# Last layer of a graph network: rows fetched by TensorE from two float32r terms, and for one block of edges in twelve

## What is computed

```python
def _L1_gnn_ref(nodes, edge_index, edge_features, mw1, mb1, uw1, ub1, uw2, ub2):
    ...
    src, dst = (edge_index[0], edge_index[1])
    msg_in = jnp.concatenate([nodes[src], edge_features], axis=1)
    messages = jax.nn.silu(msg_in @ mw1 + mb1)
    aggregated = jax.ops.segment_sum(messages, dst, num_segments=nodes.shape[0])
    upd_in = jnp.concatenate([nodes, aggregated], axis=1)
    updated = jax.nn.silu(upd_in @ uw1 + ub1) @ uw2 + ub2
    return nodes + updated
```

## Time and profile before

| what | us |
| --- | --- |
| median of 3 runs (2949.0 to 2967.78) | 2956.99 |
| the profiled execution | 2971.23 |
| its span on the core | 2969.4 |
| from the first gather of the last layer to the end of the span | 1631.15 to 2969.4 |
| PE busy | 2340.8 (79%) |
| POOL busy | 1655.3 (56%) |
| DVE busy | 1223.4 (41%) |
| ACT busy | 1130.3 (38%) |

### The profile page before, as it was taken

How to read it: one execution, slowest core, us unless ns; L and a number is a source line. 1 busy time by engine, 2 the same in 40 slices (tenths; PEclk the granted TensorE clock), 3 DMA queues, 4 the chain that set the end, 5 groups by cost and what they waited for, 6 DMA issues and landing times.

```text
span 2969.4 us, 44554 instructions
## 1 busy us (share of the span) xinstructions
PE 2340.8 (79%) x13216; PEld 1613.7 (54%) x13216; DVE 1223.4 (41%) x4042; ACT 1130.3 (38%) x2059; POOL 1655.3 (56%) x1687
## 2 busy tenths in 40 slices
PE   1588888888788888788887477878787888887888
PEld 1143433443466675566675355646565666655665
DVE  8766666666222225234434233323332332333332
ACT  4755555555565665566664211111111111111111
POOL 4566666663666663565550665555655555555553
PEclk9599999998898899799998568888978887789787
DMA  4477777675566674566673333323333332333331
GB/s 115 170 239 256 244 233 247 230 247 204 176 214 208 205 218 142 173 212 214 207 219 118 110 90 86 85 82 88 87 86 88 84 89 82 84 91 88 84 87 41
DMA packets 269705, 447.23 MB, mean 151 GB/s; under 512 B 34372, under 2 KB 219143, under 8 KB 262807
## 3 DMA queue, kind: packets, MB, share of 16 engines
q1 hardware_dynamic: 205672, 265.63, 29.3%
q0 software_dynamic: 56592, 116.00, 14.0%
q10 hardware_dynamic: 7200, 62.72, 5.4%
HBM read 363.79 MB, written 80.42 MB: 150 GB/s over the span
## 4 chain that ended last, share of the span: by engine, by line
PE 61%; another core or an unknown queue 11%; issue 11%; DVE 9%; ACT 5%; DVEq 2%; ACTq 1%; DMA 0%; POOL 0%; POOLq 0%
PE bank L1151 15%; PE bank L1206 14%; PE bank L1101 8%; PE bank L1183 6%; PE bank L1159 6%; PE bank L1120 4%; ACT shared L929 2%; PE bank L1123 1%; DVE region L1642 1%; ACT unit L572 1%; PE bank L1299 1%; DVEq L1593 1%; DVEq L1614 1%; PE bank L1104 1%
## 5 line engine op out<-in xcount | busy, mean ns | idle before, releaser
L843 POOL DMA_INDIRECT gath<-table,src_sb x1593 | 1554.9, 976 | 1121.4 <-issue 500.7
L1151 PE MATMUL bank<-unit,halves 128*128 128x500 f32 x1960 | 569.6, 435 | 111.8 <-ACT unit L572 57.8
L1597 DVE TENSOR_TENSOR acc<-acc,bank 128x31 f32 (+1 forms) x548 | 105.4, 192 | 1254.4 <-remote 747.2
L572 ACT CAST unit<-region 128x500 fp32r<-128x500 f16 x840 | 458.8, 606 | 243.8 <-PE bank L1151 190.7
L1151 PEld LDWEIGHTS bank<-unit,halves 128*128 128x128 f32 x1960 | 380.1, 207 | 226.3 <-ACT unit L572 81.4
L929 ACT CAST shared<-bank 128x490 f32 x600 | 373.6, 623 | 251.9 <-PE bank L1123 161.9
L1206 PE MATMUL bank<-shared,parts 128*128 128x384 bf16 x1890 | 406.9, 361 | 78.9 <-issue 66.7
L1038 ACT ACTIVATE region<-region 128x384 f32<-128x384 f32 x260 | 135.0, 523 | 782.1 <-DVE region L1718 622.4
L1159 PE MATMUL bank<-region,parts 128*128 128x500 f16 x1176 | 333.6, 393 | 22.2 <-DVE dense_sum L1608 15.5
L1101 PEld LDWEIGHTS bank<-onehot,region 128*128 128x128 f32 x1662 | 274.7, 231 | 135.3 <-issue 69.1
L1101 PE MATMUL bank<-onehot,region 128*128 128x31 f32 x1662 | 259.9, 293 | 100.1 <-ACT region L1038 53.0
(11 more groups left out here) (171 smaller groups left out, 1989.1 us busy)
## 6 DMA issues: line engine op xcount, KB each, us to landing
region<-counts SPq DMA_DIRECT2D x196, 875.0 KB
counts<-shared ACTq DMA_DIRECT2D x50, 1225.0 KB
region<-in_edge_T SPq DMA_DIRECT2D x138, 384.0 KB
gath<-table,src_sb POOLq DMA_INDIRECT x1593
table<-shared SPq DMA_DIRECT2D x36, 256.0 KB, 2.3
table<-parts SPq DMA_DIRECT2D x12, 384.0 KB, 2.6
shared<-in_src_row SPq DMA_DIRECT2D x17, 192.0 KB
acc<-in_x SPq DMA_DIRECT2D x12, 256.0 KB, 5.4
```

The lines of the kernel that those rows point to most:

```text
L572: copy(units[h][:, :].rearrange("p (b n) -> p b n", b=RG), ring[:, q, :, h * G:(h + 1) * G]).then_inc(done, 1)
L843: pool.indirect_dma_start(out=(gath if l > 0 else gath_parts)[:, BT * place + j, :], out_offset=None, in_=table[l], in_offset=bass.Indirec ...
L1151: mm = nc.tensor.matmul(sum_bank(ordinal), halves[:, hi, a, :], units[h][:, :], start=(hi == 0 and a == 0), stop=(hi == NTILE - 1 and a == 1))
```

## The change

It concerns the last layer. The table in SBUF becomes `halves`: two float32r terms in place of three bfloat16 ones. The first is the value with its low 12 bits masked off, made by DVE (`u_mask`) and copied by ACT (`u_high`), the second the rest, made by DVE (`u_low`); ACT's second rounding goes. A tile takes two matmuls instead of three. The one-hot matrices become float32r too, twice as large, in a ring of 13 slots instead of 28. `OWN` is every twelfth block from 36 on: 21 blocks, each in 9 ticks, five or six tiles in a tick. DVE builds matrices one tick ahead (`own_at(n + 1)`) instead of two. The silu is taken in place: `pre` and `msg` are one buffer of five blocks, not two of four. To make room, several buffers move to other places in SBUF (`shared`, `wl`, `wr`, `msg`), and `chunk_zero` in the layer before gets a wait for sums that come just before it in DVE's own order.

```diff
-NPRE = 4
+NMSG = 5
...
-OWN_FIRST, OWN_EVERY = 36, 15
+OWN_FIRST, OWN_EVERY = 36, 12
...
-OWN_TICKS = 12
-HOT_SLOTS = 28
+OWN_TICKS = 9
+HOT_SLOTS = 13
...
+        msg = over("msg", [P, NMSG, BT, D], F32, units_at[0])
...
+        hots = [over(f"hot{x}", [P, EB], F32R, shared_at + 4 * EB * x if x < SHARED_SLOTS else tail_at + 4 * EB * (x - SHARED_SLOTS)) for x in range(HOT_SLOTS)]
...
-                            after(sp, st[0]["rest_ready"], NCH + c - 1 if c > 1 else 0)
+                            after(sp, st[0]["parts_ready"], NCH + c - 1 if c > 1 else 0)
...
-                    def u_first(c):
+                    def u_high(c):
                         n = JC if c < NCH - 1 else JL
-                        act.wait_ge(xin_filled[c % 2], 16 * (X_FILLS[c % 2] + c // 2) + 16)
-                        nc.scalar.copy(parts[:, c * JC:c * JC + n, 0, :], xin[:, c % 2, 0:n]).then_inc(st[0]["part0_ready"], 1)
+                        act.wait_ge(st[0]["rest_ready"], NCH + c + 1)
+                        nc.scalar.copy(halves[:, c * JC:c * JC + n, 0, :], z_rows[:, c % 2, 0:n]).then_inc(st[0]["part0_ready"], 1)
...
-                    for a in range(3):
-                        mm = nc.tensor.matmul(bank[7][:, 0:EB], parts[:, h, a, :], own_hot(k, h), start=(h == 0 and a == 0),
-                                              stop=(h == NTILE - 1 and a == 2))
+                    for a in range(2):
+                        mm = nc.tensor.matmul(bank[7][:, 0:EB], halves[:, h, a, :], own_hot(k, h), start=(h == 0 and a == 0),
+                                              stop=(h == NTILE - 1 and a == 1))
...
-                    after(dve, msg_ready, POOLED[m - NPRE] + 1 if m >= NPRE else 0)
-                    nc.vector.tensor_tensor(pre[:, m % NPRE], edge_bank(n)[:, 0:BT * D],
+                    after(dve, block_summed, BLOCKS_BEFORE[3] + n - NMSG + 1)
+                    nc.vector.tensor_tensor(msg[:, n % NMSG].rearrange("p t d -> p (t d)"), edge_bank(n)[:, 0:BT * D],
...
-                        for k, j in own_at(n + 2):
+                        for k, j in own_at(n + 1):
                             own_hots(k, j)
```

More of the change, by code:

```diff
@@ L302, in gnn_kernel @@
         UNIT = -(-4 * RG * G // 32) * 32
+        shared_at = place(2 * 2 * NTILE * G)
         units_at = [place(UNIT) for _ in range(3)]
+        wl_at, wr_at = place(4 * 3 * D), place(4 * 3 * D)
         arena = sb("arena", [P, (placed[-1] - arena_at) // 4])
@@ L313, in gnn_kernel @@
         iota_h = sb("iota_h", [P, KS], F16)
-        wl = sb("wl", [P, 3, D])
-        wr = sb("wr", [P, 3, D])
+        wl = over("wl", [P, 3, D], F32, wl_at)
+        wr = over("wr", [P, 3, D], F32, wr_at)
         mw = sb("mw", [P, 2, D])
@@ L389, in gnn_kernel @@
         SHARED = 2 * NTILE * G
-        shared = sb("shared", [P, SHARED], F16)
+        shared = over("shared", [P, SHARED], F16, shared_at)
         stage = shared[:, :].rearrange("p (g h w) -> p g h w", g=2, h=NTILE)
@@ L395, in gnn_kernel @@
         ROWS = 4
[L398 to L401, removed]
         own_high = shared[:, 8192:8192 + EB]
@@ L1033, in _ @@
                             act.wait_ge(pre_ready, m + 1)
[L1034 removed]
                         if n in OWN:
[L1036 to L1039 removed]
+                            after(act, block_summed, BLOCKS_BEFORE[3] + n - NMSG + 1)
+                            nc.scalar.copy(msg[:, n % NMSG], bank[7][:, 0:EB].rearrange("p (t d) -> p t d", t=BT)).then_inc(msg_ready, 1)
+                        else:
+                            nc.scalar.activation(msg[:, n % NMSG], msg[:, n % NMSG], ACT.Silu).then_inc(msg_ready, 1)
                 if l < 2:
@@ L1662, in _, with u_mask, u_low @@
                         turn_unit(dve, nc.vector.tensor_copy, l, BY_DVE, units_by_dve)
-                def u_rest(c):
+                def u_mask(c):
                     n = JC if c < NCH - 1 else JL
-                    dve.wait_ge(st[0]["part0_ready"], NCH + c + 1)
+                    dve.wait_ge(xin_filled[c % 2], 16 * (X_FILLS[c % 2] + c // 2) + 16)
+                    after(dve, st[0]["part0_ready"], NCH + c - 1 if c > 1 else 0)
                     after(dve, st[0]["parts_ready"], NCH + c - 1 if c > 1 else 0)
-                    nc.vector.tensor_tensor(z_rows[:, c % 2, 0:n], xin[:, c % 2, 0:n], parts[:, c * JC:c * JC + n, 0, :],
-                                            ALU.subtract).then_inc(st[0]["rest_ready"], 1)
-                def u_third(c):
+                    nc.vector.tensor_scalar(z_rows[:, c % 2, 0:n].bitcast(I32), xin[:, c % 2, 0:n].bitcast(I32), -(1 << LOW_BITS), None,
+                                            ALU.bitwise_and).then_inc(st[0]["rest_ready"], 1)
+                def u_low(c):
                     n = JC if c < NCH - 1 else JL
-                    dve.wait_ge(st[0]["part1_ready"], NCH + c + 1)
-                    nc.vector.tensor_tensor(parts[:, c * JC:c * JC + n, 2, :], z_rows[:, c % 2, 0:n], parts[:, c * JC:c * JC + n, 1, :],
+                    dve.wait_ge(st[0]["rest_ready"], NCH + c + 1)
+                    nc.vector.tensor_tensor(halves[:, c * JC:c * JC + n, 1, :], xin[:, c % 2, 0:n], z_rows[:, c % 2, 0:n],
                                             ALU.subtract).then_inc(st[0]["parts_ready"], 1)
@@ L1732, in chunk_zero @@
                     dve.wait_ge(st[3]["z_mm"], k + 1)
+                    after(dve, added, BLOCKS_BEFORE[2] + summed)
                     end = NA if c == NCH - 1 else (c + 1) * CH
@@ L1848, in _ @@
                         if 3 <= n < NCH + 3:
-                            u_third(n - 3)
-                        if 1 <= n < NCH + 1:
-                            u_rest(n - 1)
+                            u_low(n - 3)
+                        if 2 <= n < NCH + 2:
+                            u_mask(n - 2)
                         for k, j in own_at(n + 3):
```

28 lines of the change are left out of this document (11 added, 17 removed).

## The result

The changed kernel takes **2992.53 us** (median of 11 runs, 2972.84 to 3006.27) against 2954.71 for the kernel before (11 runs, 2948.72 to 2967.78): a ratio of 1.0119, 95% interval 1.0092 to 1.0147. It is 38 us slower, where 52 us faster was forecast. Its profiled execution took 2985.26 us, only 14 above that of before: it is among the four fastest of its own runs, while before's 2971.23 is above all eleven of the other kernel.

A forecast was written before the change was run, and what follows sets the result against it. TensorE's pace was taken to bound the last layer's fetched-row stretch; -58 + 2 - 11 + 14 = -53, rounded to -52 us, gave a profiled execution near 2919 and a median near 2905, range 2857 to 2970.

The forecast's parts named there:

- Own matmuls, -58: TensorE, last layer: 2058 float32r matmuls, together 442 us, replace 2499 bfloat16 ones, together 500 us; saves 58 us.
- Work per own block, +2: TensorE: four more own blocks each bring an edge product and three transposes, less edge products saved; costs 2 us.
- VectorE, +14: VectorE's longer matrices bring message n after 3.1 us, TensorE arrives after 3.28; new waits in some ticks cost 14 us.
- the cover of 0.2 us: Own tick at 2.4 GHz: margin between VectorE's message, ready after 3.1 us, and TensorE's arrival at it after 3.28.
- The unexplained gaps, -11: TensorE's 137 us of gaps without a visible wait go with its instruction packets; 3.7 packets fewer save 11 us.
- Rival 1: Last layer: with 13 slots, 47 slow stretches each end in a message wait, 33 us together; -20, median 2937; chance 0.16.
- Rival 4: Last layer: gathers bound it, so only 12 gathers at 1.26 us are saved, -15 us, median 2942; chance 0.06.
- The signs named in advance: Profile after: forecast wrong if waits for ScalarE pass some 80 us or clock falls below 0.78; packets about 106.
- PHASE: Theory recorded for the experiments: an own cycle is two TensorE packets, so late places hit the same bad spots; 64-instruction shift changes 20 us or more.

The follow-up runs named there:

- third group: Freeing signal made late every fourth own tick: kernel before 2376.57 us, changed kernel 2654.5, changed with features first 2531.62, before with 10 slots one tick ahead 2649.7.
- f3: Changed kernel with the high term of the own rows alone, 1029 own matmuls instead of 2058: 2362.83 us, ratio to the kernel before 0.9951.
- s1: Kernel before with every twelfth block own in nine ticks, still three bfloat16 terms and 28 slots: 2367.37 us, ratio 0.9960.
- f0: The changed kernel, unaltered, run beside the kernel before on a later chip: 2367.63 us, ratio 0.9963.
- t1: Changed kernel with features and addition ahead of own matrices, and every tenth block own in seven ticks: 2473.96 us, ratio 1.0426 to the kernel before.

## Why the prediction was wrong, point by point

- **Own matmuls, -58**: right. Busy time fell by 60 us. The trace has the stream at the forecast pace, ten in 1.98 us at 2.4 GHz.
- **Work per own block, +2**: too small to be read.
- **VectorE, +14**: the local working was right and the use of it was the error. The matrices run at the pace of the earlier trace rows, five in 1.43 us, so 0.27 apart, not at that of the earlier trace rows. The Trainium skill, page "Vector Engine (DVE) Microarchitecture Reference", section 5.1, lets a one-source instruction within SBUF use both ports in such a shape; the trace agrees, with matrices 0.27 us apart where the rate of line 572 would give 0.51. The tick is as long as forecast too: from one sum to the next, 2004.26 to 2007.43, it takes 3.17 us with ten own matmuls, by the prediction's terms 0.59 + 0.75 + 1.78 = 3.12. But the cover of 0.2 us was checked against a signal of 0.1 us after the matmul, the value of an undisturbed tick. The term charged 14 us of new waits; the trace has 180.
- **The unexplained gaps, -11**: this is the step that failed. I wrote that the gaps go with the instructions "since they stand in no wait", and took them as TensorE's own. They are the part that shows of something larger. In the same stretches TensorE's signals come late, by up to some 14 us, and before TensorE seldom had to wait for what hung on them (61 us), because 28 slots and two ticks held matrices and messages for that long. The earlier trace rows pointed there: VectorE's rows beside it show 9.8 us of idle time, and I read TensorE's alone. The change took the cover away: gaps 137 to 57, waits for ScalarE 61 to 241. That is -80 and +180, together +100, where this term and VectorE's had -11 and +14, together +3. How much of the +100 is the shorter cover alone and how much the new places of the late signals stays open.
- **Rival 1** had the mechanism and its place, and mis-sized the price: 0.7 us at 47 stretches, 33 us, since it allowed a wait of 3.1 us less TensorE's remaining work. The wait is the lateness less that work. Measured, it is 241 us in 54 waits (43 and 11), up to 13.3 us each, so 4.5 us a wait.
- **Rival 4** was refuted in this trace (324.8 us of GpSimd's waits), and is what happens where no signal is late: -15 us with features first, -8 as it is. The chain that ended last names it there; for the changed kernel on the first chip, then on a later one:

```profile
PE 50%; another core or an unknown queue 17%; DVE 13%; issue 10%; ACT 5%; DVEq 3%; DMA 1%; ACTq 0%; POOL 0%; POOLq 0%
```

```profile
PE 34%; POOL 27%; issue 12%; DVE 5%; DMA 4%; ACT 2%; DVEq 1%; POOLq 0%; ACTq 0%
```

- **The signs named in advance**: "wrong if waits for ScalarE grow past some 80 us" came true at 241. The clock stayed (0.81) and 107 packets came for 106.

Open: whether the order alone (features first) or 28 slots with float32r would win back the 38 us on the first chip. By the third group features first wins back two fifths of the loss from late slots. PHASE: the late places do fall on few spots of the own cycle in the changed kernel's trace (around its 170th, 310th and 450th to 470th of some 500 matmuls and loads, the last of them 10 to 14 us long), where before they lie scattered, and the shift by 64 instructions changed nothing where nothing is late; on the first chip it wasn't tried. So PHASE stands as a rival there, for a part of the loss.

## What to carry to other kernels

The slots of a ring are cover against late signals and not spare memory: before halving them, list what each waiting engine would do if the signal that frees a slot came 5 to 10 us late, and check it in the slow places of the trace, not in the clean tick. A gap that "waits for nothing" on one engine calls for a look at the others' waits for that engine in the same microseconds. And a saving on an engine that is 80 to 90% busy counts only after asking what goes at its own pace behind it: here 1029 matmuls could go (f3) or 588 come (s1) without moving the time by more than 10 us. The verdict itself hung on the chip: 38 us slower on one, 8 us faster on another.

## What the runs showed of the hardware

- TensorE's semaphore updates may come 2.5 to some 14 us behind the matmuls that carry them, with later matmuls running (129 places over 2.5 us in the whole program before, 125 after; on the later chips none). The chain of waits shows it as time of an unknown queue: 17% of the changed kernel's span on the first chip, 11% of that of before, and no such share in the changed kernel's on a later chip. What delays them isn't settled. It isn't a low granted clock at the start: in the last layer the clock is still 2.4 GHz when the matmul ends in 60 of the 67 places before and in 55 of the 62 after, and 1.2 GHz when the signal comes in 45 and in 26. It isn't the kernel alone either, since the changed kernel shows none on a later chip.
- The same program took 2955 us on one chip and 2375 on four others. The gathers' own pace (1.25 us) is the same on both, and VectorE's busy time within 2% in the changed kernel; the difference is in waits and in TensorE.
- TensorE's granted clock in the last layer differs from kernel to kernel on the later chips: 0.80 with 787 us busy of 984 (f3), 0.87 with 892 (f0), 0.96 with 946 (s1), but also 0.96 with 913 of 1090 (t1), so the busy time alone doesn't tell it. From f0 to f3, 1029 matmuls less were only 106 us of busy time less, 0.10 us each, where they run 0.17 apart at 2.4 GHz.
